# Row-by-row fetches by SyncE in place of three gathers, and products in units of 64 samples, in a recommendation-model kernel

## The reference

```python
e = jnp.stack([tbl_0[ids[:, 0]], ..., tbl_25[ids[:, 25]]], axis=1)      # 2048 x 26 x 128
sd = jnp.einsum('bfd,bd->bf', e, dense)
ss = jnp.einsum('bfd,bgd->bfg', e, e)
z = jnp.concatenate([dense, sd, ss[:, iu, ju]], axis=1)                # iu, ju: the pairs above the diagonal
h = jnp.concatenate([z, dense], axis=1)
h = jnp.maximum(h @ W_top1 + b_top1, 0.0)                              # 607 x 512
h = jnp.maximum(h @ W_top2 + b_top2, 0.0)                              # 512 x 256
y = h @ W_top3                                                         # 256 x 1
```

## Time and profile before

| What | us |
|---|---|
| Median of 3 runs of the kernel before | 378.31 |
| Lowest and highest of them | 378.00, 378.87 |
| Span of the profiled execution, first to last instruction | 376.5 |
| TensorE busy in it | 347.3 (92%) |
| GpSimd busy in it | 267.1 (71%) |
| VectorE busy in it | 252.4 (67%) |
| ScalarE busy in it | 187.5 (50%) |
| Idle before the gathers, for the cause "issue" | 80.5 |

### The profile page before, as it was taken

One profiled execution on the slowest core, in us unless ns is written; L12 is line 12 of the kernel. 1 busy time (PEld: TensorE's weight loads), 2 busy tenths in 40 slices (PEclk: granted clock), 3 DMA queues, 4 the chain that ended last, 5 costly groups with the idle time before them and its releaser, 6 DMA issues.

```text
span 376.5 us, 12740 instructions
## 1 busy us (share of the span) xinstructions
PE 347.3 (92%) x5585; PEld 273.7 (73%) x5585; DVE 252.4 (67%) x501; ACT 187.5 (50%) x320; POOL 267.1 (71%) x279
## 2 busy tenths in 40 slices
PE   2899988999799999998999999986899999989987
PEld 0566666876578888876788888864678778779876
DVE  0799899886589735787788646884588672545241
ACT  3356777677113426767323347574214345524443
POOL 6777778777777777777777777777777777877200
PEclk9999999999899999999999999999899999969999
DMA  7998114333242332333432331342243221122100
GB/s 191 256 256 201 51 49 106 94 85 112 67 111 77 85 84 57 86 88 97 111 81 84 78 91 51 87 119 71 75 104 91 51 62 51 52 51 52 31 4 1
DMA packets 20111, 33.43 MB, mean 89 GB/s; under 512 B 7917, under 2 KB 10491, under 8 KB 20057
## 3 DMA queue, kind: packets, MB, share of 16 engines
q0 software_dynamic: 8704, 17.84, 18.4%
q1 hardware_dynamic: 11353, 14.78, 15.0%
HBM read 32.60 MB, written 0.01 MB: 87 GB/s over the span
## 4 chain that ended last, share of the span: by engine, by line
PE 70%; POOL 13%; issue 7%; DMA 5%; DVE 4%; ACT 1%; SPq 0%; DVEq 0%; ACTq 0%; POOLq 0%
POOL rows L552 13%; PE late_bank L576 10%; PE late_bank L664 10%; PE gram_bank L616 8%; PE late_bank L577 8%; PE turn_bank L597 6%; DMA rows<-in_tbl_dram,index 4%; PE gram_bank L576 3%; PE spare_bank L710 3%; PE gram_bank L577 3%; PE spare_bank L576 2%; PE spare_bank L880 2%; PE spare_bank L577 2%; PE turn_bank L577 1%; PE turn_bank L576 1%
## 5 line engine op out<-in xcount | busy, mean ns | idle before, releaser
L552 POOL DMA_INDIRECT rows<-in_tbl_dram,index x272 | 266.3, 979 | 83.9 <-issue 80.5
L1115 DVE TENSOR_TENSOR one_hot<-table_ids,row_number 125x512 fp32r<-125x512 int32 x216 | 134.8, 682 | 30.8 <-PE gram_bank L577 13.1
L403 ACT COPY turned<-turn_bank 128x512 f32<-128x512 f32 (+1 forms) x69 | 68.3, 1033 | 49.0 <-PE turn_bank L597 49.0
L576 PE MATMUL late_bank<-one_hot,table_hi 125*128 125x512 f32 x168 | 72.1, 429 | 1.9 <-DVE one_hot L1113 1.0
L577 PE MATMUL late_bank<-one_hot,table_lo 125*128 125x512 f32 x168 | 67.6, 403 | 0.0
L616 PEld LDWEIGHTS gram_bank<-turned 128*27 128x27 f32 x4096 | 45.3, 106 | 18.7 <-issue 14.1
L616 PE MATMUL gram_bank<-turned 128*27 128x26 f32 x4096 | 55.0, 193 | 2.3 <-DVE turned L417 1.4
L597 PE MATMUL turn_bank<-ident,rows 128*128 128x128 f32 x288 | 44.1, 277 | 12.5 <-DMA rows<-in_tbl_dram,index 11.5
L597 PEld LDWEIGHTS turn_bank<-ident,rows 128*128 128x128 f32 x288 | 35.1, 143 | 23.0 <-DMA rows<-in_tbl_dram,index 14.2
L576 PEld LDWEIGHTS late_bank<-one_hot,table_hi 125*128 125x128 f32 x168 | 32.5, 194 | 16.5 <-issue 5.3
L1113 DVE TENSOR_SCALAR one_hot<-looked_up,row_number_sb 125x512 fp32r<-125x512 f32 x72 | 32.8, 496 | 11.5 <-issue 6.3
(11 more groups left out here) (138 smaller groups left out, 460.5 us busy)
## 6 DMA issues: line engine op xcount, KB each, us to landing
table_ids<-in_ids_by_table_dram SPq DMA_DIRECT2D x27, 256.0 KB, 3.3
rows<-in_tbl_dram,index POOLq DMA_INDIRECT x272
turned<-in_tbl_dram SPq DMA_DIRECT2D x6, 448.0 KB, 12.1
looked_up<-in_tbl_dram SPq DMA_DIRECT2D x3, 448.0 KB, 5.6
rows<-in_r_dense_features_dram SPq DMA_DIRECT2D x16, 64.0 KB, 3.2
gram<-in_W_top_dram SPq DMA_DIRECT2D x1, 702.0 KB
gram<-in_W_top_dram SPq DMA_DIRECT2D x1, 512.0 KB
turned<-in_tbl_dram SPq DMA_DIRECT2D x6, 52.0 KB
```

What stands on the lines that cost most here:

```text
L403: copy(to[:, f0:f1], of).then_inc(rows_copied[n % 2], 1)
L552: pool.indirect_dma_start(out=rows[:, row % RING_ROWS, :], out_offset=None, in_=tables[f], in_offset=bass.IndirectOffsetOnAxis(ap=index[:, ...
L576: pe.matmul(bank, table_hi[:, s, k, :], hot, start=k == 0, stop=False)
L1115: last = nc.vector.tensor_tensor(hot, table_ids[0:RK, (chunk.n * LOOKUPS + s) % ID_SLOTS, 0:wide], row_number[0:RK, k:k + 1].broadcast_to( ...
```

## The change

Two things are changed.

1. The gathers of the 17th gathered feature (table 24, 1250 rows) of tiles 9, 12 and 15 leave GpSimd's list. SyncE fetches these 3 x 128 rows one by one, each with a plain transfer whose address comes from a register, into a buffer of their own (`fetched`). It loads the three lists of ids into one partition of SBUF, in the room of `gram` after the low parts of the weights are made, and then in each step loads 8 ids into registers and issues 8 transfers of 512 bytes. There are 48 steps. Twelve are put between the other loads of each of the first three chunks (two or three before the ids of look-up 2, then one or two between each load and the next), the last twelve after the dense rows of tile 15. The turn of group 4 of such a tile waits for all 128 rows.
2. In the first three chunks, a call of products makes 16 groups of 4 (64 samples) instead of 8, at u = 0 and u = 2; VectorE copies the first of a tile, ScalarE the second. The last chunk stays as it was.

```diff
+WIDE = 2
+FETCHED = {9: 17, 12: 17, 15: 17}
+FETCH_STEP = 8
+FETCHES = len(FETCHED) * P // FETCH_STEP
+FETCHES_A_CHUNK = 12
+def wide(chunk):
+    return 1 if chunk is LAST else WIDE
+        fetched = sb("fetched", [P, len(FETCHED), D])
+        fetched_ids = late_room[ACROSS:ACROSS + 1, 0:len(FETCHED) * P].bitcast(I32).rearrange("p (i r) -> p i r", r=P)
...
+            unit = UNIT * wide(chunk)
+            of = gram_bank[mine][0:ACROSS, 0:unit * LATER].rearrange("p (k f) -> p k f", k=unit)
...
+            def load_fetched_ids():
+                sp.wait_ge(w2_lo_made, 1)
+                sp.wait_ge(w1_lo_made, K1)
+                for i, (tile, f) in enumerate(FETCHED.items()):
+                    sp.dma_start(fetched_ids[:, i], ids_t[GATHERED[f - 1]:GATHERED[f - 1] + 1, tile * P:(tile + 1) * P]
+                                 ).then_inc(fetched_ids_loaded, DMA)
+            def fetch_rows(steps):
+                for n in steps:
+                    i, first = divmod(n * FETCH_STEP, P)
+                    table = tables[GATHERED[list(FETCHED.values())[i] - 1]]
+                    if n == 0:
+                        sp.wait_ge(fetched_ids_loaded, len(FETCHED) * DMA)
+                    _, numbers = nc.values_load_multi_w_load_instructions(
+                        fetched_ids[0:1, i, first:first + FETCH_STEP], engines=(mybir.EngineType.SP,), min_val=0,
+                        max_val=table.shape[0] - 1, skip_runtime_bounds_check_because="they are row numbers of the table")
+                    for r, number in enumerate(numbers, first):
+                        sp.dma_start(fetched[r:r + 1, i, :], table[bass.ds(number, 1), :]).then_inc(rows_fetched[i], DMA)
...
+                step = chunk.n * FETCHES_A_CHUNK
                 load_ids(following, 0)
                 load_ids(following, 1)
+                if chunk is CHUNKS[0]:
+                    load_fetched_ids()
+                fetch_rows((step,))
+                fetch_rows((step + 1,))
                 load_dense(ahead)
+                fetch_rows((step + 2,))
                 load_ids(following, 2)
+                fetch_rows((step + 3,))
                 load_dense(ahead + 1)
                 load_ids(following, 3)
+                fetch_rows((step + 4,))
                 load_ids(following, 4)
+                fetch_rows((step + 5,))
                 load_dense(ahead + 2)
+                fetch_rows((step + 6,))
                 load_ids(following, 5)
+                fetch_rows((step + 7,))
                 load_dense(ahead + 3)
+                fetch_rows((step + 8,))
                 for s in range(LATE, LOOKUPS):
                     load_ids(following, s)
+                    fetch_rows((step + 3 + s,))
             for n in range(LAST.first + RING_TILES, tiles):
                 load_dense(n)
+            fetch_rows(range(len(CHUNKS[:-1]) * FETCHES_A_CHUNK, FETCHES))
             store_rows()
...
+                    if FETCHED.get(t) == n + 1:
+                        continue
...
-                    pe.wait_ge(gathered[i][g], times * DMA * (f1 - f0 - (g == 0)))
+                    pe.wait_ge(gathered[i][g], DMA * gathers_until(tile, g))
+                    if f0 <= FETCHED.get(tile, -1) < f1:
+                        pe.wait_ge(rows_fetched[list(FETCHED).index(tile)], P * DMA)
...
-                        products(chunk, t, u)
+                        if u % WIDE == 0:
+                            products(chunk, t, u // WIDE)
...
-                        if u % 2:
-                            copy_products(act, chunk, t * UNITS + u)
+                        if u == WIDE:
+                            copy_products(act, chunk, t * UNITS // WIDE + 1)
...
-                        if u % 2 == 0:
-                            copy_products(dve, chunk, t * UNITS + u)
+                        if u == 0:
+                            copy_products(dve, chunk, t * UNITS // WIDE)
```

More of the change, by code:

```diff
@@ L129, in turn_range, with gathers_until, products_before @@
     return g * TURN, min((g + 1) * TURN, ROWS)
+def gathers_until(tile, g):
+    f0, f1 = turn_range(g)
+    return sum(1 for t in range(tile % RING_TILES, tile + 1, RING_TILES) for f in range(max(f0, 1), f1) if FETCHED.get(t) != f)
 def turns_before(u):
     return range(-(-u * TURNS // UNITS), min(-(-(u + 1) * TURNS // UNITS), TURNS))
+def wide(chunk):
+    return 1 if chunk is LAST else WIDE
+def products_before(tile):
+    return min(tile, LAST.first) * UNITS // WIDE + max(tile - LAST.first, 0) * UNITS
 def turns_until(row):
@@ L255, in dlrm_tower @@
         ids_loaded = [sem(f"ids_loaded{s}") for s in range(LOOKUPS)]
+        fetched_ids_loaded = sem("fetched_ids_loaded")
+        rows_fetched = [sem(f"rows_fetched{i}") for i in range(len(FETCHED))]
         gathered = [[sem(f"gathered{i}_{g}") for g in range(TURNS)] for i in range(RING_TILES)]
@@ L369, in copy_products @@
                 engine.wait_ge(w1_lo_made, K1)
-            engine.wait_ge(gram_done, chunk.first * UNITS + n + 1)
-            of = gram_bank[mine][0:ACROSS, 0:UNIT * LATER].rearrange("p (k f) -> p k f", k=UNIT)
+            engine.wait_ge(gram_done, products_before(chunk.first) + n + 1)
+            unit = UNIT * wide(chunk)
+            of = gram_bank[mine][0:ACROSS, 0:unit * LATER].rearrange("p (k f) -> p k f", k=unit)
             room = n % (HALF * UNITS) if chunk is LAST else n
-            copy(gram[0:ACROSS, room * UNIT:(room + 1) * UNIT, :], of).then_inc(gram_copied[mine], 1)
+            copy(gram[0:ACROSS, room * unit:(room + 1) * unit, :], of).then_inc(gram_copied[mine], 1)
         def copy_cols(engine, part, g):
@@ L412, in place_found @@
             if t >= 2:
-                engine.wait_ge(gram_done, (chunk.first + t - 1) * UNITS)
+                engine.wait_ge(gram_done, products_before(chunk.first + t - 1))
             to = turned[:, t % 2].rearrange("p i (q f) -> p f q i", q=GROUP)[:, ROWS:FEATURES]
@@ L596, in turn_rows @@
                     for f in range(f0, f1):
-                        last = pe.transpose(turn_bank[n % 2][:, f - f0, :], rows[:, (tile * ROWS + f) % RING_ROWS, :], ident[:])
+                        of = rows[:, (tile * ROWS + f) % RING_ROWS, :]
+                        if FETCHED.get(tile) == f:
+                            of = fetched[:, list(FETCHED).index(tile), :]
+                        last = pe.transpose(turn_bank[n % 2][:, f - f0, :], of, ident[:])
                     last.then_inc(rows_turned, 1)
@@ L609, in products @@
                         pe.wait_ge(found_placed, chunk.first - chunk.n + t)
-                n = t * UNITS + u
-                pe.wait_ge(gram_copied[n % 2], UNITS + (chunk.first * UNITS + n) // 2)
-                for k in range(UNIT):
+                unit = UNIT * wide(chunk)
+                n = t * (GROUPS // unit) + u
+                pe.wait_ge(gram_copied[n % 2], UNITS + (products_before(chunk.first) + n) // 2)
+                for k in range(unit):
                     for q in range(GROUP):
-                        sample = turned[:, t % 2, u * UNIT + k, q * FEATURES:(q + 1) * FEATURES]
+                        sample = turned[:, t % 2, u * unit + k, q * FEATURES:(q + 1) * FEATURES]
                         last = pe.matmul(gram_bank[n % 2][q * QUAD:q * QUAD + FEATURES, k * LATER:(k + 1) * LATER],
@@ L624, in turn_products @@
                     for i in range(2):
-                        pe.wait_ge(gram_copied[i], UNITS + (part.first + part.tiles) * UNITS // 2)
+                        pe.wait_ge(gram_copied[i], UNITS + products_before(part.first + part.tiles) // 2)
                 if part.tiles == TILES:
```

## The result

The kernel became slower: 384.52 us (median of 5 executions, 383.74 to 385.98) against 378.26 for the kernel before (5 executions, 377.16 to 378.87), a ratio of 1.0176, with a 95% interval from 1.0156 to 1.0195. Forecast were 375.8 us and "faster"; the time lies in the range, on its slower side. The profiled execution has a span of 382.57 us, 6.0 more than before (376.55). The ratios further down, unlike the medians, leave out executions more than 1.5% above the fastest of their kernel: three of ten of the changed kernel with tile 15's gather back on GpSimd (all above 381.7, so its ratio is lower than its median suggests), one of ten of the one with two steps moved, and one of the kernel before (1675.95 us, beside the first four experiments).

A forecast was written before the change was run, and what follows sets the result against it. GpSimd's gathers were taken to bound the kernel, TensorE following. Span 376.5 less 2.5 for gathers, with merged calls and SyncE's fetches at 0, gives 374.0; plus 1.8 for the median, 375.8 us, range 373.6 to 387.

The forecast's parts named there:

- GpSimd as the metronome: GpSimd's gathers, 1.25 us each, set the pace; two fewer before tile 14's last gather are worth 2.5 us, not 3.75.
- The gathers behind tile 14: After tile 14's turn, moved to 328.7, no gather binds; tile 15's come 3.75 us earlier where 2.5 are needed.
- The late ids: Chunk 0: look-up 2's ids go out at 78.5, not 69.4; TensorE loses up to 3 us, cost at the end 0.
- A step on SyncE: Loading 8 row numbers and issuing 8 one-row transfers takes 3.8 us, from 2.95 to 6.1.
- the point from which it decides: SyncE's last 12 steps have 49.65 us before tile 15's turn; above 4.14 us a step they are late.
- The 5.0 us a step: Estimate for a SyncE step from the skill's page: 0.43 us a transfer, 0.6 a load; the sum would be 388.
- units of 64 samples: Products in the first three chunks: merging 24 pairs of calls saves 0.19 us each, 4.6 us; worth 0 at the end.
- TensorE does not get the time back: Rival: steps late by just the gain, later gathers, slower merged products or look-up stalls give 377.6 to 379; gain eaten, chance 0.11.
- the cover: Time saved by merged calls lengthens TensorE's waits for gathers, over 11.5 us in sum, and can absorb delays from SyncE's fetches.
- the start of SyncE's last 12 steps: They follow tile 15's dense rows, which went out at 301.35; with 1.25 and 0.6 us gained, 299.5.
- SyncE comes too late for tile 15: Rival at the turn at 353.35: costs 12 x (step - 4.14), plus 1.7 us of clock after longer waits; chance 0.35.
- The clock: TensorE: half clock after a wait of some us costs 1.7 us; rival, clock stays high: 374.1 or 372.4, chance 0.08.

The follow-up runs named there:

- the first four experiments: Against the kernel before: row fetches only, 375.51 us; 64-sample calls only, 379.70; only tiles 9 and 12 fetched, 375.63; three plain block transfers instead, 375.38.
- The two experiments with this late end removed: Against the changed kernel: two of SyncE's last 12 steps put ahead of tile 15's dense rows, 378.13 us; tile 15's gather back on GpSimd, 380.32 us.

## Why the prediction was wrong

**Right.** *GpSimd as the metronome*: its gathers kept 1.25 us from start to start (345.34 and 346.59 in the kernel after), and with calls of 32 two fewer ahead of tile 14 were worth 2.3 to 2.8 us by the ratios of three kernels (0.9938, 0.9934, 0.9926), not 3.75. *The gathers behind tile 14*: two instead of three changed nothing in the times (375.63 and 375.51 us), though one trace has 0.82 us of waiting for tile 15's. *The late ids* of look-up 2: issued at 80.56 instead of the 78.5 forecast. With calls of 32 the stall was 3.4 us where 3 were forecast, with 6.8 us at half clock, and the waits for gathers took it up; in the kernel after TensorE came too late to notice it.

**A step on SyncE.** The instructions of the row transfers (L548) and of the load of 8 numbers (L544) in the kernel after: count, then ns at least, median and at most:

```profile
L548 SPq FUSED_REGOPS  x384: 37/37/47, 68.1 to 357.9; - x192
L548 SPq MOVE fetched<-in_tbl_dram x384: 29/29/38, 68.2 to 357.9; - x192
L548 SPq DMA_DIRECT2D fetched<-in_tbl_dram x384: 224/228/299, 68.2 to 358.0; - x192
```

```profile
L544 SPq TENSOR_LOAD <-gram x48: 717/744/848, 67.3 to 354.1; - x48
```

The transfer with an address from a register takes 0.228 us, as the one-partition row had it (0.244); the load 0.744 instead of 0.9; but a row has two register instructions, not one. The 12 steps from 307.75 to 358.22 are 4.21 us each, where 3.8 were taken and 4.14 was the point from which it decides. The term was 0.4 too small, 4.9 us over 12 steps. It did not decide by itself: alone, with the start at 298 and a landing of 1.0 us behind the last issue instead of 1.7, SyncE was late by 0.3 us.

The Trainium skill, "DMA: Bandwidth & Descriptors", Latency and other measured facts, has some 600 ns for the register load; the 744 ns agree in size. The same page's table on issuing has 512 sequencer cycles for a transfer before the newest generation, by estimate 0.43 us at 1.2 GHz, and the 384 transfers here took 0.228 each: the measurement decides. The 5.0 us a step that the prediction estimated from the page did not come.

**The step that failed: units of 64 samples**, "0.19 us a pair of calls saved, 4.6 us in 24 ... Worth at the end: 0", with the pace of a call taken over from the earlier trace rows. The doubt was named, "below nothing, if twice as many short instructions behind each other drain TensorE's queue", but got no term in the sum; "products that run slower merged" stood as one clause of the rival *TensorE does not get the time back*, which ended at 379. Measured: 9.2 us lost in the calls and 1.9 in waits for one-hots. Nothing is left of the cover: the waits for gathers, 11.5 us before, were to grow and are gone, and TensorE is 4.4 us late at tile 14's turn besides, instead of 2.5 early. Of these 15.9 us the calls and one-hots explain 11.1. Tile 0 was turned 1.3 us later (58.14 against 56.88), ahead of the first merged call: in the kernels profiled it came between 56.84 and 58.61. The last 3.5 us are not traced to a cause. There were four half-clock stretches ahead of 331 (at 87.0, 155.3, 240.6, 267.9), where before there were two (97.9, 265.15) and the beginning of one at 330; two more of 3.4 us can cost up to 1.7 us each, but some of it falls into the calls and is counted there already.

**What followed from it.** The 2.5 us of the gathers were not collected, since no gather was waited for. And the start of SyncE's last 12 steps, 299.5 in the sum, hangs on TensorE: the dense rows of tile 15 wait for a turn of tile 12, which came at 306.8, where before it came at 300.7. The sum had the right limit (50 us for 12 steps) and took its start as given. So the rival *SyncE comes too late for tile 15* is what happened at the end of the kernel, but through its start, not its price: 8 us later at the start, 2.95 us of waiting at the end, since tile 15's turn was late itself. The two experiments with this late end removed come back to 378.1 and 380.3; the one with the merged calls' hold removed as well (the calls cut, the copies moved) to 374.9.

**The clock.** For a wait of some us the prediction added 1.7 us. After the wait of 2.95 the granted clock did go to 0.50, the 1.2 GHz level, from 360.1 to 363.5:

```profile
360.10:363.50 3.40, 3.40 (x136) 2.59 (x135) 0.37 (x1) 1.08 (x4) 0.00 (x0) 0.50 0.02 5
```

(Columns as the earlier trace rows.) But from tile 15's turn to the end the kernel after took 23.31 us, and at full clock the one before took 23.20 and the changed kernel with two steps moved 22.93: 0.1 to 0.4, not 1.7. TensorE was busy for 19.88 us in it against 18.92 before; it is idle between dependent layers in this part, and most of the slower products fit into that time. Even where it was busy without a break, between tile 14's turn and tile 15's, 5.6 us at half clock went with only 1.4 us more than at full clock.

## What to carry to other kernels

A saving in one engine's list counts as cover only after its new order has been priced; a run of short instructions twice as long is a new operation, not two of the old. Of a helper that works just in time, find what starts its last piece of work, and put that work ahead of the wait, not behind it: moving two steps of 48 took back 6.4 us by the medians. And a copy of a unit twice as long waits twice as long, with everything queued behind it, so it moves to where its unit is done.

## What the runs showed of the hardware

**Long runs of short matmuls are not fed without gaps.** In each merged call, 128 weight loads of 27 columns and 128 products of 26, TensorE pauses for 0.1 to 0.4 us, mostly twice or three times and at changing places, and in four to six calls of the 24 for 0.7 to 2.2 us (in the kernel after at 76.8, 84.3, 172.0, 179.5 and 265.1). Of the 48 calls of 64 products in the kernel before, 28 have a short pause inside, of 0.2 us at most, and none a long one. The long pauses are bound to a place in TensorE's list, not to a time: in all six kernels with 128 products on end, each one above 0.6 us comes after product 112 of the third call or 87 of the fourth in chunk 0, 108 of the fourth or 79 of the fifth in chunk 1, 101 of the fifth or 80 of the sixth in chunk 2; four of these six places have one in every kernel. The instruction queue of the page's third part brings 44 packets of 16 KB:

```profile
q8 instruction: 44, 0.72, 0.8%
```

At each of the five long pauses such a packet was under way or had ended at most 0.5 us earlier; at 84.3 it took from 83.72 to 84.68, and the pause went from 84.26 to 86.20. That the two belong together is suggested by this and by the fixed places, but not tested by itself: packets also came within calls without a long pause (69.69 to 70.63), and why a pause outlasts the packet by 1.5 us stays open. The Trainium skill, "Runtime: NRT & Kernel Launch", Instruction fetch mechanics, has the fetch hidden behind the sequencer's pace of issue; for the calls of 32 samples in the kernel before the trace agrees (0.3 us in two waits without a releaser), for 256 short instructions in a row 7.5 to 8.4 us of pauses without a releaser speak against it, or for another cause than the fetch.

**A row with its address from a register** costs SyncE 0.41 us: 0.228 for the transfer, 0.066 for two register instructions, and the gaps between them; 8 numbers are loaded in 0.744 us, and a turn that had to wait for its last row started 1.0 us after that row's issue had ended (1.04 and 1.03 us in two kernels).

**Start-up wobbles by 1.8 us.** Tile 0's last turn came between 56.84 and 58.61 in the kernels profiled, one execution of each; mostly later in those with transfers to `fetched` (57.55 to 58.61, one at 56.90) than in the others (56.84 to 57.13, one at 57.63). Where TensorE waits for gathers later on, such a delay can be taken up; where TensorE sets the end, it can't. That would fit the wider scatter of two kernels with merged calls and rows fetched (375.96 to 382.76) beside the kernel before (377.11 to 379.68, in the same group), but it is argued, not shown.
